# Memory keys and values projected pair by pair, weights stationary, in the second attention of a two-layer block

## The reference, cut to what matters

```python
xn = (x - mu) * rsqrt(var + EPS) * ln_g + ln_b
q = _split_heads(xn @ Wq)                       # 16 heads of 64
kv = xn @ Wkv
k = _split_heads(kv[..., :INNER]); v = _split_heads(kv[..., INNER:])
mem = _split_heads(memories @ Wm)               # memories = ctx_1024, Wm 512 x 1024
k = concatenate([k, mem], axis=2)               # 100 own + 722 memory rows
v = concatenate([v, mem], axis=2)               # the same rows again
attn = softmax(einsum('bhid,bhjd->bhij', q, k) * DIM_HEAD ** -0.5)
out = einsum('bhij,bhjd->bhid', attn, v)        # then @ Wo + bo, and x + that
```

## Time and profile before

| | |
|---|---|
| median of 3 runs | 1912.72 us |
| the profiled execution | 1913.55 us, span 1911.9 us |
| busy in the span | PE 88%, PEld 71%, DVE 56%, ACT 41%, POOL 7% |
| mean granted TensorE clock | 0.934 |
| first matmul of `attend` to end of its last output | 806.7 to 1502.9 us |
| PE busy in 844.5 to 1421.4 us | 561.35 of 576.90 us |

### The profile page before, as it was taken

How to read it: one execution, slowest core, us unless ns; L and a number is a source line. 1 busy time by engine, 2 the same in 40 slices (tenths; PEclk the granted TensorE clock), 3 DMA queues, 4 the chain that set the end, 5 groups by cost and what they waited for, 6 DMA issues and landing times. The chain is left out here.

```text
span 1911.9 us, 31342 instructions
## 1 busy us (share of the span) xinstructions
PE 1673.1 (88%) x11296; PEld 1354.9 (71%) x11296; DVE 1078.0 (56%) x1840; ACT 776.3 (41%) x1400; POOL 136.2 (7%) x177
## 2 busy tenths in 40 slices
PE   5996359999999689899999999999998719999993
PEld 5775359999999389567676766767665519999981
DVE  5775547667767543135554545555465326766765
ACT  2453135555555132134443434444354115445440
POOL 4000310000000301100000000000000040000004
PEclk9998579999999889899999999999999659999997
DMA  9300265565566344231111111111100065655634
GB/s 339 137 9 1 80 227 204 204 213 197 200 209 227 84 149 147 79 103 29 38 28 39 29 32 41 28 38 28 27 14 6 1 216 177 216 211 191 216 138 123
DMA packets 98510, 223.45 MB, mean 117 GB/s; under 512 B 36696, under 2 KB 57304, under 8 KB 83324
## 3 DMA queue, kind: packets, MB, share of 16 engines
q1 hardware_dynamic: 82988, 175.72, 28.1%
q0 software_dynamic: 15440, 46.56, 7.0%
HBM read 180.61 MB, written 41.62 MB: 116 GB/s over the span
## 5 line engine op out<-in xcount | busy, mean ns | idle before, releaser
L955 DVE TENSOR_TENSOR e_lo<-e_raw,e_hi 128x2048 fp32r<-128x2048 f32 x118 | 270.2, 2290 | 128.7 <-ACT e_hi L1018 128.7
L918 PE MATMUL banks<-e_xh,e_hi 128*128 128x256 f32 x1024 | 292.5, 286 | 12.3 <-DVE e_xl L971 7.5
L918 PE MATMUL banks<-e_xl,e_hi 128*128 128x256 f32 x1024 | 291.8, 285 | 0.0
L918 PE MATMUL banks<-e_xh,e_lo 128*128 128x256 f32 x1024 | 291.7, 285 | 0.0
L1593 PE MATMUL banks<-a_wm,a_ch 128*128 128x512 f32 (+1 forms) x768 | 248.0, 404 | 22.3 <-DVE a_v L1721 11.3
L1018 ACT CAST e_hi<-e_raw 128x2048 fp32r<-128x2048 f32 x118 | 224.7, 1904 | 70.2 <-PE banks L935 28.6
L918 PEld LDWEIGHTS banks<-e_xh,e_hi 128*128 128x128 f32 x1024 | 197.9, 193 | 20.8 <-issue 8.3
L918 PEld LDWEIGHTS banks<-e_xl,e_hi 128*128 128x128 f32 x1024 | 197.9, 193 | 5.5
L918 PEld LDWEIGHTS banks<-e_xh,e_lo 128*128 128x128 f32 x1024 | 197.9, 193 | 0.0
L1593 PEld LDWEIGHTS banks<-a_wm,a_ch 128*128 128x128 f32 (+1 forms) x768 | 134.0, 183 | 61.8 <-issue 15.6
L1767 DVE COPY a_PT<-banks 128x200 f32<-128x200 f32 x128 | 46.5, 363 | 189.0 <-PE banks L1638 188.8
(11 more groups left out here) (234 smaller groups left out, 2674.6 us busy)
## 6 DMA issues: line engine op xcount, KB each, us to landing
e_raw<-wout SPq DMA_DIRECT2D x50, 1024.0 KB, 4.9
e_raw<-w SPq DMA_DIRECT2D x34, 1024.0 KB, 4.9
e_raw<-wgate SPq DMA_DIRECT2D x17, 1024.0 KB
e_raw<-wup SPq DMA_DIRECT2D x17, 1024.0 KB, 4.8
a_craw<-ctxT SPq DMA_DIRECT2D x40, 256.0 KB, 2.9
e_xs<-slot_rows SPq DMA_DIRECT2D x18, 512.0 KB
slot_outs<-e_y POOLq DMA_DIRECT2D x16, 512.0 KB, 3.2
slot_rows<-a_zero POOLq DMA_DIRECT2D x15, 512.0 KB, 10.3
```

What stands on the lines that cost most here:

```text
L918: mm = nc.tensor.matmul(ps[:, bank, 0:CAP], w[:, cc, cut], x[:, cc, :], start=t == 0, stop=t == len(terms) - 1)
L955: nc.vector.tensor_tensor(lo[g % 2][i][:], raw[q % RAW][:], hi[g % 2][i][:].bitcast(F32), ALU.subtract)\
```

## The change

Each pair of heads gets its own projection. The stationary operand is the pair's 128 columns of Wm, the moving one the context, 362 and then 360 rows: 24 matmuls a pair (`memory`, two halves, banks 6 and 7). The result is the keys' layout at once; ACT copies the first half to `kT`, DVE the second. `turn_values` transposes six blocks of `kT` to get the values, and ACT copies them to `v`, now one buffer of 128 columns for each of four slots. In step p PE computes the scores of pair p, one turn of pair p - 1, half the projection of pair p + 2, the other turn, the other half, the transposes for the values of pair p + 1, and the heads of pair p - 1.

The context is split by feature chunk: four chunks of 128 features by 722 rows, four `craw` buffers, and `ch`, `cl` for a whole batch, twice. Chunk cc of batch b + 1 is loaded and split in step m = 1 + cc of batch b. Own values are loaded pair by pair. How a head's turned probabilities are copied (five blocks by ACT, two by DVE) is as it was; only its place in the order of DVE and ACT moves.

The diff, cut to its core:

```diff
 def attend(k, s1):
...
-    SPLIT = {0: (1, 2), 1: (1, 3), 2: (1, 4), 3: (1, 5), 6: (2, 0), 7: (2, 1)}
+    HALF = [(0, 362), (362, S - 362)]
+    SPLIT_AT = {1 + cc: cc for cc in range(DC)}
...
+        craw = s1.craw + [k.sb(c, f"a1_craw{u}", [128, S]) for u in range(2, DC)]
+        ch = [k.sb(c, f"a1_ch{u}", [128, DC, S], F32R) for u in range(2)]
+        cl = [k.sb(c, f"a1_cl{u}", [128, DC, S], F32R) for u in range(2)]
...
             def _(sp):
+                def context(b, cc):
+                    after(sp, cl_done, DC * (b - 1) + cc + 1)
+                    sp.dma_start(craw[cc][:], a["ctxT"][bass.ds(b, 1), 128 * cc:128 * cc + 128, :]
+                                 .rearrange("b p s -> p (b s)")).then_inc(craw_in[cc], 16)
+
+                def own(b, m):
+                    b, m = b + m // IC, m % IC
+                    p, s = IC * b + m, m % SLOTS
+                    if not exists(p):
                         return
+                    after(sp, sc, p - SLOTS + 1)
                     sp.dma_start(q[s][:], s1.q[bass.ds(b, 1), :, m, :].rearrange("b p t -> p (b t)"))\
                         .then_inc(qk_in[s], 16)
                     sp.dma_start(kT[s][:, 0:T], s1.kk[bass.ds(b, 1), :, m, :].rearrange("b p t -> p (b t)"))\
                         .then_inc(qk_in[s], 16)
+                    after(sp, yd, p - SLOTS + 1)
+                    sp.dma_start(v[s][0:T, 0, :], s1.v[bass.ds(b, 1), :, 128 * m:128 * m + 128]
+                                 .rearrange("b t n -> t (b n)")).then_inc(v_in[s], 16)
+
+                for cc in range(2):
+                    sp.sem_inc(craw_in[cc], 16)
+                for cc in range(2, DC):
+                    context(0, cc)
                 for m in range(SLOTS - 1):
                     own(0, m)
                 sp.dma_start(s1.wo[:], a["Wo"].rearrange("(c p) n -> p c n", p=128)).then_inc(o_in, 16)
                 sp.dma_start(bo[:], a["bo"].partition_broadcast(T)).then_inc(o_in, 16)
-                for nb in range(3, NB + 4):
-                    context(0, nb)
-                def step(b, u, m, left):
-                    if left >= 0:
-                        own(b, m + SLOTS - 1)
-                    if m in SPLIT and left >= SPLIT[m][0]:
-                        context(b + SPLIT[m][0], SPLIT[m][1] + 2)
-                    if m == 1 and left >= 1 and not (type(b) is int and b == 0):
-                        own_values(b + 1, 1 - u)
+
+                def step(b, u, m):
+                    own(b, m + SLOTS - 1)
+                    if m in SPLIT_AT and later(b):
+                        context(b + 1, SPLIT_AT[m])
...
+                def memory(p, b, u, m, half, first=False):
+
+                    if half == 0:
+                        after(pe, k_a, p)
+                        after(pe, ys, p - 3)
                     else:
+                        after(pe, k_v, p)
+                    start, wide = HALF[half]
+                    for cc in range(DC):
+                        if m == 0 and half == 0:
+                            pe.wait_ge(cl_done, DC * b + cc + 1)
+                        cut = slice(128 * m, 128 * m + 128)
+                        for t, (w, x) in enumerate(((s1.wm[0], ch[u]), (s1.wm[0], cl[u]), (s1.wm[1], ch[u]))):
+                            mm = nc.tensor.matmul(ps[:, 6 + half, 0:wide], w[:, cc, cut], x[:, cc, start:start + wide],
+                                                  start=cc == 0 and t == 0, stop=cc == DC - 1 and t == 2)
+                    mm.then_inc(pj, 1)
...
+                def turn_values(p, m):
+
+                    pe.wait_ge(k_a, p + 1)
+                    pe.wait_ge(k_v, p + 1)
+                    if exists(p - 2):
+                        pe.wait_ge(pt_a, 2 * (p - 1))
+                        pe.wait_ge(pt_v, 2 * (p - 1))
+                    else:
+                        after(pe, v_done, p)
                     for nb, (first, size) in enumerate(MB):
+                        mm = nc.tensor.transpose(ps[0:size, 4 + nb // 4, 128 * (nb % 4):128 * (nb % 4) + 128],
+                                                 kT[m % SLOTS][:, first:first + size], k.ident[:])
+                    mm.then_inc(vt, 1)
...
                 def turn(p, m, two):
+                    pe.wait_ge(pn, 2 * p + two + 1)
+                    if two == 0:
+                        after(pe, v_done, p + 2 if exists(p + 1) else p + 1)
+                    else:
+                        pe.wait_ge(pt_a, 2 * p + 1)
+                        pe.wait_ge(pt_v, 2 * p + 1)
                     for n, (first, size) in enumerate(KB1):
                         mm = nc.tensor.transpose(ps[0:size, 4 + n // 5, T * (n % 5):T * (n % 5) + T],
                                                  P[(2 * m + two) % 4][:, first:first + size], k.ident[0:T, 0:T])
                     mm.then_inc(pt, 1)
...
+                def attended(p, b, m):
+                    s = m % SLOTS
+                    pe.wait_ge(pt_a, 2 * p + 2)
                     pe.wait_ge(pt_v, 2 * p + 2)
+                    pe.wait_ge(v_done, p + 1)
+                    pe.wait_ge(v_in[s], 16 * (2 * b + m // SLOTS + 1))
+                    if exists(p + 3):
+                        pe.wait_ge(k_a, p + 4)
+                    else:
+                        pe.wait_ge(ys, p)
...
+                def step(b, u, m):
+                    p = IC * b + m
+                    scores(p, b, m)
+                    prev = exists(p - 1)
+                    if prev:
+                        turn(p - 1, back(b, m)[1], 0)
+                    memory_ahead(b, u, m, 0)
+                    if prev:
+                        turn(p - 1, back(b, m)[1], 1)
+                    if m == OUTPUT_AT + 1:
+                        after(pe, os_, b)
+                    memory_ahead(b, u, m, 1)
+                    if exists(p + 1):
+                        turn_values(p + 1, (m + 1) % IC)
+                    if prev:
+                        attended(p - 1, *back(b, m))
+                    if m == OUTPUT_AT and exists(p - IC):
+                        output(b - 1, 1 - u)
+
+                for half in range(2):
+                    memory(0, 0, 0, 0, half)
+                for half in range(2):
+                    memory(1, 0, 0, 1, half)
...
             @block.vector
             def _(dve):
...
+                def split(b, u, cc):
+                    dve.wait_ge(ch_done, DC * b + cc + 1)
+                    nc.vector.tensor_tensor(cl[u][:, cc, :], craw[cc][:], ch[u][:, cc, :].bitcast(F32), ALU.subtract)\
+                        .then_inc(cl_done, 1)
...
+                    dve.wait_ge(pj, 2 * p + 2)
+                    start, wide = HALF[1]
+                    nc.vector.tensor_copy(kT[m % SLOTS][:, T + start:T + start + wide], ps[:, 7, 0:wide])\
+                        .then_inc(k_v, 1)
...
+                def step(b, u, m):
                     p = IC * b + m
+                    highest(p, m, 0)
                     if exists(p - 1):
                         turned(p - 1, (m - 1) % IC, 0)
+                    highest(p, m, 1)
+                    normalise(p, m, 0)
                     if exists(p - 1):
                         turned(p - 1, (m - 1) % IC, 1)
+                    normalise(p, m, 1)
+                    if exists(p + 2):
+                        keys(p + 2, (m + 2) % IC)
+                    if m in SPLIT_AT and later(b):
+                        split(b + 1, 1 - u, SPLIT_AT[m])
+                    if m == OUTPUT_AT and exists(p - IC):
+                        add_output(b - 1)
...
             @block.scalar
             def _(act):
...
+                def split(b, u, cc):
+                    act.wait_ge(craw_in[cc], 16 * b + 16)
+                    nc.scalar.copy(ch[u][:, cc, :], craw[cc][:]).then_inc(ch_done, 1)
...
+                def values(p, m):
+                    act.wait_ge(vt, p + 1)
+                    to = v[m % SLOTS]
+                    nc.scalar.copy(to[:, 1:5, :].rearrange("p n d -> p (n d)"), ps[:, 4, :])
+                    nc.scalar.copy(to[:, 5:7, :].rearrange("p n d -> p (n d)"), ps[:, 5, 0:256]).then_inc(v_done, 1)
...
+                def step(b, u, m):
                     p = IC * b + m
                     if exists(p - 1):
                         turned(p - 1, (m - 1) % IC, 0)
+                    exponent(p, m, 0)
+                    exponent(p, m, 1)
                     if exists(p - 1):
                         turned(p - 1, (m - 1) % IC, 1)
+                    if exists(p + 2):
+                        keys(p + 2, (m + 2) % IC)
+                    if exists(p + 1):
+                        values(p + 1, (m + 1) % IC)
+                    if exists(p - 1):
+                        attended(p - 1, u if m >= 1 else 1 - u, (m - 1) % IC)
+                    if m in SPLIT_AT and later(b):
+                        split(b + 1, 1 - u, SPLIT_AT[m])
...
```

(41 more changed lines are left out.)

280 lines of the change are left out of this document (63 added, 217 removed).

## The result

The changed kernel takes 1961.03 us (median of 4 runs, 1957.45 to 1962.3), the kernel before in the same job 1912.1 (4 runs, 1910.17 to 1913.72): ratio 1.0253, 95% interval 1.0236 to 1.0271. The profiled run took 1960.68 us, its span is 1959.0, which is 47.1 more than before. Two executions in what follows, one of experiment 4 and one of the kernel before in the second job, took 2473 and 2498 us at a mean granted clock of 0.64 and are left out of medians and ranges.

The account below looks back on a forecast made before the run. PE's own work was taken to bound the attention stage; from the profiled 1913.6 us, - 28 for the stage without stalls, + 60 for stalls and + 24 for clock falls gave 1970, median 1969, range 1940 to 2000.

Parts of the forecast that it names:

- The wait: Attention stage: late row loads stall PE's second turn of probabilities by 2.75 us in 22 steps, 60 us in all.
- lead-in: Attention stage from first matmul to first scores: as long as Wo and bo take to arrive, 15.7 us.
- the step: A full step of the attention stage, PE's parts added without waits: 9.27 us, 61 of them 565.5 us.
- the chain: Heads' end releases value load, then row load, ACT's cast, DVE's subtraction, maximum, turned copy, PE's second turn: 2.75 us stall.
- The clock: PE's granted clock falls behind two of three of the 22 stalls, 1.1 us on average: 24 us.
- The rival of a stall without a fall: Attention stage: the stalls come but PE's clock holds: 1945 us, chance 0.24.
- Load pace: Stage's projections on PE: weight loads lie beside 361-column matmuls, a group of 12 takes 2.10 us, 2.16 an upper side.
- The base: Attention stage without stalls and clock falls: 668 us for 696.2, 28 us less.
- two turns at 0.69: In each full step PE's two turns of probabilities, seven transposes each, were counted at 0.69 us apiece.
- balance: The change gains by spreading projections over steps, not by 12 groups ahead of first scores and none in the last batch.
- faster, loads in time: Rival: row loads arrive in time and PE runs 9.27 us steps: 1885 us, chance 0.07.
- The rival of 0.19 us a matmul: Each projection matmul costs its weight load's 0.19 us instead of 0.168: 33 us more, 2002, chance 0.04.

Follow-up runs that it names:

- experiment 4: Changed kernel with eight value buffers instead of four, so the value load waits for heads of seven pairs ago: 1868.52 us, ratio 0.9773.
- experiment 1: Changed kernel with the row load issued ahead of the pair's own loads in each step of the DMA queue: 1870.0 us, ratio 0.9787.
- experiment 2: Changed kernel with ACT's and DVE's halves of the split one step later, loads where they were: 1869.79 us, ratio 0.978.
- experiment 3: Changed kernel with only DVE's subtraction of the split one step later: 1893.62 us, ratio 0.9906.
- experiment 10: experiment 3 with a second ACT cast of each row chunk, into an unread buffer, ahead of the real cast: 1916.95 us, ratio 1.0022.
- experiment 8: experiment 1 with each half projection in two column parts, twice as many matmuls and weight loads: 1968.84 us, ratio 1.0288.
- experiment 5: experiment 1 with the loop's edge moved from behind step 7 to behind step 1, after the output projection: 1859.73 us, ratio 0.9738.
- experiment 7: Changed kernel, loads in their late order, with only the loop's edge moved behind step 1: 1950.3 us, ratio 1.0182.
- experiment 9: experiment 8 with the loop's edge moved behind step 1: 1954.96 us, ratio 1.0216.
- experiment 11: experiment 5 with DVE copying all seven blocks of a head's turned probabilities, ACT none: 1866.3 us, ratio 0.9759.

## Why the prediction was right

**The wait: right, in place, number and size.** In the steps ACT's cast waited for rows 28 times, 3.0 to 3.9 us each and 98 in all, where 28 times and some 100 were predicted; two waits in the lead-in make it 100.5. PE's second turn waited in 22 steps, 2.10 to 2.98 us each. Inside the loop the value and the row load go at 0.24 and 0.80 to 0.82 us into the step, where 0.24 and 0.79 stood in the working; in batch 0, ahead of the loop, at 0.11 and 0.46. The rows were cast 2.84 to 3.49 us behind their load, 3.11 on average, where 3.2 was taken. The turn was due at 4.22 instead of 4.35 and starts at 6.94 on average instead of 7.10. With the 0.18 of the visible end, 22 x 2.74 = 60.3 us, against 60: the chain is right in every link, and luck has its part in an agreement to the tenth, since start and due time were both put some 0.15 too late. The delayed steps lasted 11.2 to 14.6 us, for 12 to 13.6. Experiments 1, 2 and 4 remove the wait in three independent ways (queue order, time of use, the awaited buffer), and their medians lie within 1.5 us of each other.

**The clock: right, in size and frequency.** 17 falls of 22 where two of three were taken, 1.55 us each and 2.86 once instead of 1.6: 27.7 us against 24. The rival of a stall without a fall (1945) is out for these waits; experiment 3 shows stalls without falls, but of 0.39 to 1.32 us. The reason given, that these stalls are longer than the 2.34 us one of the kernel before, is not enough: waits of 2.11 to 2.65 us had no fall in 5 steps, and in experiment 10 one of 1.81 had.

**Load pace: right.** Undelayed matmuls of 361 columns start 0.165 us apart; experiment 8 finds the load's own pace below that, at 0.11. The Trainium skill's figure for a load (TensorE: Matmul & The Clock Gate, LDWEIGHTS) is columns/1.2 ns, 107 ns for 128 columns; as a pace of loads that lie beside matmuls it agrees with the 0.11. As a cost on the path ahead of each matmul it would by my estimate have made the half of experiment 8 4.4 us (24 x (0.107 + 0.075)); it took 2.73.

**The base: two errors that partly cancel.** Without waits the stage was to be 28 us shorter. Of the 47.1 us measured, 60.3 + 27.7 are the waits and falls, so the base is 40.9 shorter, 39.8 of it in the stage (744.4 for 696.1 us). Step by step:
- the step: 8.93 us, not 9.27. In experiment 1 the halves take 2.07 (predicted 2.10), but the two turns 0.59 and 0.54, not 0.69. The working took only 0.07 us off the visible 0.76 of seven transposes; a turn followed by a projection starts it 0.2 us before its visible end. 61 steps: - 21;
- lead-in 14.0 instead of 15.7 (its last wait, 0.50 us, ends with the landing of bo, as predicted), step 0 6.4 for 6.7, tail 22.5 for some 23, step 62 9.3 for 8.1: - 1;
- the loop's edges, not foreseen: 4.95 and 5.10, together + 10.

28 + 22 - 10 = 40. So the sum of 1970 for the profiled execution, against 1960.7, is 9 too high: 13 by the base, less 4 by the clock. What failed was the step's "two turns at 0.69", and that the list of what the change moves left out the loop's jump and what PE has queued ahead of it.

Is it balance that the change gains? About half. In the profile of experiment 5, without waits and edges, the stage is 52.8 us shorter than before: 24.3 in the lead-in (13.5 for 37.8), 4.9 in batch 0, and 5.4 in each of batches 1 to 6 (78.5 for 83.9), less 8.4 in the last batch and its tail (89.9 for 81.5). The working had the same signs, with 22 in the lead-in, 2 in batch 0, 2.7 in each full batch and 12 lost in the last. Of the 5.4 us of a full batch the halves make 1.2 (16 x 2.07 for 12 x 2.86); the rest was not taken apart.

The rivals: "faster, loads in time" was made by experiment 1, at 1870 where 1885 stood in the working; the 15 us are the same base. The rival of 0.19 us a matmul fell with experiment 8.

## What to carry to other kernels

An in-order DMA queue passes a wait on to every load behind it: a load that several steps could cover is late when it stands behind one that waits for the current step's last work. Before looking at what a reordering saves, write down for each load the event that lets its queue reach it. And when a loop is rewritten, look at what the busiest engine has queued ahead of the jump: 7 us hid it here, 1.4 us left 3.3 us of idle and, but for one edge, a slow stretch behind it. Nothing between was tried.

## What the runs showed of the hardware that was not expected

- The jump of a loop left PE idle for 3.0 to 3.5 us at all 14 edges behind the heads in seven profiles (changed kernel, experiments 1, 2, 3, 4, 8 and 10), and for nothing that shows behind the output projection (kernel before, experiments 5, 7, 9 and 11).
- Idle time of PE of 1.8 to 3.4 us may or may not lower the granted clock: 2.39, 2.65 and 3.38 us did not (experiment 10, changed kernel, experiment 1), 1.81 did (experiment 10).
- Behind the gap of 3.0 to 3.5 us the lower level, where it came, lasted some 3 to 7 us with 361-column matmuls and some 17 and 20 with 182-column ones, though PE counted as busy nearly throughout. The same short matmuls, once at the full level, stayed at it (experiment 9), but its lead-in of 24.4 us passed at the lower one.
